# A two-layer graph network: layer 1 gives 25 chunks of gathered rows to the queues of SP and ScalarE instead of 38

## The chip, the cores and the metric

One core of a Trainium2 chip runs the whole program. The metric is the device time of one execution in microseconds, the median of several. The engines are TensorE (PE, matmuls), VectorE (DVE), ScalarE (ACT), GpSimd (POOL) and SyncE (SP), each with its own instruction queue, and 16 DMA engines which move what SP, ScalarE and GpSimd issue.

## The reference

3750 nodes with 256 features, 120,000 edges sorted by their target, 8 edge types. Layer 0 is a graph attention layer and layer 1 a relational one. Cut to layer 1, on which the change works:

```
h    = relu(layernorm(x))                    # 3750 x 256
W    = einsum('rb,bio->rio', comp, basis)    # 8 types
hall = einsum('ni,rio->nro', h, W)           # 30000 rows of 256 floats: tab1
msgs = hall[src, type]                       # 120000 gathered rows
agg  = segment_sum(msgs, dst)                # sum per target node
x    = x + layernorm(gelu(agg + h @ loop_w + bias + h)) * gamma + beta
```

## The kernel before

The nodes are 30 blocks of 128. The edges, sorted by target block, are cut into chunks of 128; layer 1 has `SLOTS` = 120000 // 128 + 30 = 967 chunks in groups of `G` = 32. For each chunk the 128 rows of `tab1` (1 KB each) are brought to the 128 partitions, and TensorE multiplies them with a one-hot matrix of the targets (`OH`), which sums them per target node. Chunks are taken in units of two, those from 936 on singly. After each unit VectorE adds the PSUM bank to the accumulator of the target's block (`add`, L1361), whose offset it has in a register.

Rows come in one of two ways. For most chunks GpSimd issues one indirect DMA (`fetch`, L867 to L882) into `FE`, which has room for two groups. Before every eighth chunk it waits until TensorE is done with the eight that lay there (L877), so it runs at most 56 to 64 chunks ahead. For the chunks in `BY_SP` and `BY_ACT` (L21, L22) the rows are copied one at a time by SP or ScalarE: `row_loads` (L518) loads 16 row addresses into registers with one register load (L526) and issues one DMA of 1 KB for each (L531), eight times for a chunk. They go to six tiles of their own, three for each queue (`QROWS`, named `qs` and `qa`). A chunk may be started when the one three before it in its list has been multiplied. `fetch` leaves these chunks out. TensorE takes all chunks in order and waits for each one's semaphore (L2110 to L2122).

SP does nothing but `row_loads` in this stage, all 128 rows of a chunk after those of the last (L773). ScalarE has other work between: for each node block b (one to a group of chunks) it makes `HXL` (L1826) and the next block's `relu` (`own_rows`, L1812), and then issues its share of register loads (L1829). TensorE multiplies block b with `loop_w` behind unit 11 of group b (`own_product`, chunk 24 of the group), for which it needs that `HXL`. ScalarE's first chunk is issued whole ahead of block 0's `HXL` (L1821).

Layer 0 gives chunks to the same queues by its own rule (`direct0`, `row_loads0`), which the change doesn't touch.

Of the kernel before, what the change touches and what calls it, by code (L numbers as in the profile page):

```python
# [17 lines left out]
GROUPS1 = [(k, min(G, SLOTS - k)) for k in range(0, SLOTS, G)]  # L18
UNITS = [(k, 2) for k in range(0, TWOS, 2)] + [(k, 1) for k in range(TWOS, SLOTS)]
ENT = 2 * NB + 1  # L20
BY_SP = [47 * j + 46 for j in range(20)]  # L21
BY_ACT = [52 * j + 50 for j in range(18)]  # L22
ER, EC = 125, 960
PARTS = (slice(0, 112), slice(112, ER))
EP = E + 128
# [20 lines left out]
def program(nc, x, src, dst, et, w0, al, ar, hb0, basis, comp, loopw, hb1, gam, bet, out):  # L46
# [15 lines left out]
    with ctx:  # L62
# [368 lines left out]
        def all_scored(g):  # L431

            return scored(g, halves(g) - 1)
# [29 lines left out]
        def direct(k):  # L463

            return k in BY_SP or k in BY_ACT

        def place_of(k):

            by = BY_SP if k in BY_SP else BY_ACT
            i = by.index(k)  # L470
            return 3 * (by is BY_ACT) + i % 3, i // 3

# [45 lines left out]
        def row_loads(e, engine, by, i, first, last):  # L518


            c = by[i]
            slot, use = place_of(c)
            if i >= 3 and first == 0:
                e.wait_ge(s_pair, NPAIR + unit_of(by[i - 3]) + 1)
            for p in range(first, last, 16):
                at = nc.values_load_multi_w_load_instructions(  # L526
                    ROWKEY[c % 128:c % 128 + 1, c // 128 * 128 + p:c // 128 * 128 + p + 16], engines=[engine],
                    min_val=0, max_val=4 * D * (NB * 128 * NREL - 1), skip_runtime_bounds_check_because=
                    "a key is 8 times a node plus a type, or one of the padding's below 30000, times the bytes of a row")[1]
                for r, v in enumerate(at):  # L530
                    e.dma_start(QROWS[slot][p + r:p + r + 1, :].bitcast(U8), bytes1[:, bass.ds(v, 4 * D)]).then_inc(d_q[slot], 16)  # L531
# [61 lines left out]
        def _(sp):  # L593
# [178 lines left out]
            sp.wait_ge(s_sc, all_scored(NG - 1))  # L772
            for i in range(len(BY_SP)):  # L773
                row_loads(sp, SYE, BY_SP, i, 0, 128)

# [888 lines left out]
        def _(ac):  # L1664
# [36 lines left out]
            for layer in range(2):  # L1701
# [9 lines left out]
                for j in range(4 if layer == 0 else 0):  # L1711
                    n = slice(512 * j, 512 * j + 512)
# [68 lines left out]
                for g in range(NG):  # L1781
                    k0, n = GROUPS[g]
# [25 lines left out]
            def own_rows(b):  # L1808

                if b:  # L1810
                    ac.wait_ge(s_tr, 2 * NB + b)
                ac.activation(ERM[:, 0:256], X[:, b, :], ACT.Relu, bias=nmr[:, b:b + 1], scale=rs[:, b:b + 1]).then_inc(*o.of(s_h))  # L1812
# [7 lines left out]
            ac.wait_ge(s_ef, NG)  # L1820
            row_loads(ac, SE, BY_ACT, 0, 0, 128)  # L1821
            for b in range(NB):
                ac.wait_ge(s_hm, 2 * NB + b + 1)
                if b:
                    ac.wait_ge(s_mm, 9 * NB + b)
                ac.activation(HXL[:, 0, :], ERM[:, 256:512], ACT.Copy).then_inc(*o.of(s_hi))  # L1826
                if b + 1 < NB:
                    own_rows(b + 1)
                for n in range(8 + 5 * b, min(13 + 5 * b, 8 * len(BY_ACT))):  # L1829
                    row_loads(ac, SE, BY_ACT, n // 8, n % 8 * 16, n % 8 * 16 + 16)  # L1830

            ac.activation(sm[:, 0, 0:1], ones[:, 0:1], ACT.Gelu).then_inc(*o.of())
# [325 lines left out]
```

## Time and profile before

| | us |
|---|---|
| median of 3 runs | 4180.63 (4178.63 to 4185.44) |
| the profiled execution | 4177.85 |
| its span, first to last instruction | 4175.4 |
| layer 1's first gather | 2214.6 |
| SP's last chunk of rows multiplied from | 4116.86 |

| engine | busy us | share of the span |
|---|---|---|
| PE | 1996.9 | 48% |
| PE weight load | 1520.2 | 36% |
| DVE | 1602.5 | 38% |
| ACT | 588.0 | 14% |
| POOL | 1984.0 | 48% |

Busy time doesn't count instructions that issue DMAs or load registers, so the table says nothing of SP. The mean granted TensorE clock is 0.687 of full speed.

### The profile page before, as it was taken

To read this page: it belongs to the slowest core of one execution; us is meant where nothing else is said; L and a number is where in the kernel's file an instruction comes from. 1 tells how busy PE (TensorE), PEld (TensorE's weight loads), DVE (VectorE), ACT (ScalarE), POOL (GpSimd) and SP (SyncE) were. 2 spreads that over 40 slices of the span, in tenths; PEclk is the share of its full clock that TensorE was granted. 3 is DMA by queue.
4 is the path that set the end of the run, shared out by engine and by line. 5 is a ranking of instruction groups with operands and counts; after the bars stand their busy time and mean duration, and the time that the engine had idled before them with its cause. 6 is when DMAs were issued, how large, how long until landed. Compare 5 with 4: busy or idle time off the path is not lost.

```text
span 4175.4 us, 44278 instructions
## 1 busy us (share of the span) xinstructions
PE 1996.9 (48%) x8319; PEld 1520.2 (36%) x8319; DVE 1602.5 (38%) x3360; ACT 588.0 (14%) x1181; POOL 1984.0 (48%) x2091
## 2 busy tenths in 40 slices
PE   8843555555555555555893243333233332323334
PEld 7832434333344343333682133222222222222223
DVE  6744445444544455445772122212122122211224
ACT  5332111122211122221250000000000000000003
POOL 6654555555555554554205445444344454534441
PEclk9966767666666676676896566566566666666667
DMA  8453333333333333333354222222122222222221
GB/s 237 169 184 89 104 101 102 100 91 107 105 104 103 102 104 88 102 107 86 131 184 130 65 68 77 65 69 68 51 63 72 68 75 67 74 57 61 63 68 47
DMA packets 185625, 397.95 MB, mean 95 GB/s; under 512 B 54570, under 2 KB 109666, under 8 KB 177024
## 3 DMA queue, kind: packets, MB, share of 16 engines
q0 software_dynamic: 92096, 252.73, 22.1%
q1 hardware_dynamic: 84800, 138.01, 9.9%
q10 hardware_dynamic: 8448, 4.37, 0.5%
q14 instruction: 215, 1.76, 0.1%
q8 instruction: 66, 1.08, 0.1%
HBM read 320.39 MB, written 74.55 MB: 95 GB/s over the span
## 4 chain that ended last, share of the span: by engine, by line
SPq 28%; issue 26%; PE 19%; DVE 11%; another core or an unknown queue 10%; ACTq 3%; ACT 1%; DVEq 1%; DMA 0%; POOL 0%; POOLq 0%
SPq L531 24%; PE PB L1947 9%; PE PB L1890 7%; SPq L526 4%; DVE ZX L1389 4%; DVE OHZ L1379 3%; ACTq L507 2%; DVE ACC L1361 2%; PE PB L1999 1%; DVE ERM L1370 1%; DVEq L1337 1%; PE PB L2050 0%; ACTq L502 0%; DVE EV L1405 0%
## 5 line engine op out<-in xcount | busy, mean ns | idle before, releaser
L882 POOL DMA_INDIRECT ZX<-tab,KI x1896 | 1809.3, 954 | 2012.8 <-PE PB L1947 1075.8
L1947 PE MATMUL PB<-ZX,OHZ 128*128 128x260 f32 (+1 forms) x3850 | 1221.1, 476 | 573.6 <-issue 350.4
L1361 DVE TENSOR_TENSOR ACC<-ACC,PB 128x260 f32 (+1 forms) x997 | 421.7, 423 | 2152.5 <-PE PB L1947 1012.2
L1947 PEld LDWEIGHTS PB<-ZX,OHZ 128*128 128x128 f32 x3850 | 901.6, 243 | 811.7 <-issue 404.4
L1890 PE MATMUL PB<-wh,hx 128*128 128x512 f32 (+2 forms) x980 | 308.5, 387 | 11.2 <-ACT hx L1686 5.6
L1999 PE MATMUL PB<-OHZ,ERG 128*32 128x256 bf16 x1494 | 157.5, 337 | 324.6 <-issue 313.9
L1389 DVE TENSOR_TENSOR ZX<-ZX,PB 128x2048 f32<-128x2048 f32 (+1 forms) x125 | 284.1, 2273 | 0.0
L1826 ACT ACTIVATE hxl<-ERM 128x256 fp32r<-128x256 f32 x30 | 12.5, 416 | 1881.0 <-issue 1201.4
L1999 PEld LDWEIGHTS PB<-OHZ,ERG 128*32 128x32 bf16 x1494 | 67.7, 109 | 412.2 <-issue 398.0
L1890 PEld LDWEIGHTS PB<-wh,hx 128*128 128x128 f32 x980 | 190.6, 195 | 33.9 <-ACT hx L1686 10.0
L1890 PE MATMUL PB<-wx,hx 128*128 128x512 f32 (+2 forms) x490 | 186.9, 381 | 0.0
L1754 ACT ACTIVATE OHZ<-OHZ,kid 128x4096 bf16<-128x4096 bf16 (+1 forms) x32 | 115.7, 3615 | 490.1 <-issue 444.3
L2015 PE MATMUL PB<-pick,ERM 128*128 128x16 f32 (+1 forms) x504 | 112.9, 374 | 149.7 <-DVE ERM L1370 94.7
L2015 PEld LDWEIGHTS PB<-pick,ERM 128*128 128x128 f32 (+1 forms) x504 | 109.4, 329 | 170.0 <-DVE ERM L1370 106.8
L1890 PE MATMUL PB<-wlh,hxl 128*128 128x256 f32 x120 | 40.5, 395 | 270.0 <-ACT hxl L1826 268.2
L1947 PE MATMUL PB<-qs,OHZ 128*128 128x256 f32 x40 | 21.8, 647 | 306.2 <-DMA qs<-tab 269.1
L1379 DVE TENSOR_TENSOR OHZ<-DL,PB 128x1024 f32<-128x1024 bf16 (+1 forms) x122 | 140.1, 1209 | 0.1
L1578 DVE TENSOR_TENSOR OHZ<-DL,PB 128x4096 f32<-128x4096 bf16 (+1 forms) x31 | 133.4, 4307 | 0.0
L1890 PEld LDWEIGHTS PB<-wlh,hxl 128*128 128x128 f32 x120 | 27.5, 252 | 277.8 <-ACT hxl L1826 205.6
L1947 PEld LDWEIGHTS PB<-qs,OHZ 128*128 128x128 f32 x40 | 11.3, 314 | 313.2 <-DMA qs<-tab 232.9
L2098 PE MATMUL PB<-IDX,ERM 128*128 128x128 f32 x30 | 12.0, 401 | 217.6 <-DVE ACC L1605 134.5
L1756 ACT ACTIVATE OHZ<-OHZ,ones 128x4096 bf16<-128x4096 bf16 (+1 forms) x32 | 115.7, 3615 | 1.0
(336 smaller groups left out, 1735.6 us busy)
## 6 DMA issues: line engine op xcount, KB each, us to landing
qs<-tab SPq DMA_DIRECT2D x2560, 1.0 KB
qa<-tab ACTq DMA_DIRECT2D x2304, 1.0 KB
tab<-ZX SPq DMA_DIRECT2D x34, 1024.0 KB
OHZ<-dlt SPq DMA_DIRECT2D x31, 1024.0 KB
ZX<-tab ACTq DMA_DIRECT2D x1920, 1.0 KB
ZX<-tab,KI POOLq DMA_INDIRECT x1896
ZX<-tab SPq DMA_DIRECT2D x1792, 1.0 KB
tab<-ZX SPq DMA_DIRECT2D x24, 1040.0 KB
```

Source lines behind the costliest of these rows:

```text
L526: at = nc.values_load_multi_w_load_instructions(ROWKEY[c % 128:c % 128 + 1, c // 128 * 128 + p:c // 128 * 128 + p + 16], engines=[engine], ...
L531: e.dma_start(QROWS[slot][p + r:p + r + 1, :].bitcast(U8), bytes1[:, bass.ds(v, 4 * D)]).then_inc(d_q[slot], 16)
L882: pool.indirect_dma_start(to, None, tab, at).then_inc(d_fe[g % 2][part(g, k) * layer], 16)
L1361: dv.tensor_tensor(a, a, bank(done + i)[:, 0:width], ALU.add).wait_op(*previous, "sem-ge").then_inc(*o.of(s_add))
L1379: dv.tensor_tensor(OH[:, 0, c:c + w, :], DL[:, k0 + c:k0 + c + w].unsqueeze(2).to_broadcast([128, w, 128]), (iob[:, :] if c and g == NG - ...
L1389: dv.tensor_tensor(f, f, weights.unsqueeze(3).to_broadcast([128, w, 4, HD]), ALU.mult).then_inc(*o.of(s_sr))
L1578: dv.tensor_tensor(OH[:, g % 2, 0:n, :], DL[:, k0:k0 + n].unsqueeze(2).to_broadcast([128, n, 128]), lanes.unsqueeze(1).to_broadcast([128, ...
L1754: ac.activation(d, d, ACT.Abs, bias=kid[:, 0:1], scale=-1.0).then_inc(*o.of())
L1890: last = pe.matmul(to, hx[:, 128 * c:128 * c + 128], parts[u](c), start=(i == 0 and c == 0 and u == 0), stop=(i == 1 and c == 1))
L1947: last = pe.matmul(p, OH[:, slot, k + i, :], rows_, start=(i == 0), stop=(i == n - 1))
L1999: last = pe.matmul(PB[2 + half][32 * a:32 * a + 32, 256 * (m % 2):256 * (m % 2) + 256], ERG[:, q, 32 * i:32 * i + 32], DLB[:, g % 2, 2 * q ...
L2015: last = pe.matmul(to, ERM[0:32 * parts, 128 * j:128 * j + 128], pick[0:32 * parts, 0:4 * parts].rearrange("p (a h) -> p a h", h=4), start ...
```

## The change

`BY_SP` has 13 chunks, 69, 141, ... 933, where it had 20 (46, 93, ... 939); `BY_ACT` has 12, 56, 132, ... 892, where it had 18 (50, 102, ... 934). The 13 chunks that neither list holds any more are fetched by GpSimd, 942 gathers instead of 929. ScalarE's register loads of 16 rows are dealt out to the blocks at three and four in turn instead of five; its first chunk is still issued ahead of block 0. All else, the tiles and the rules for waits among it, follows from the two lists.

```diff
-BY_SP = [47 * j + 46 for j in range(20)]
-BY_ACT = [52 * j + 50 for j in range(18)]
+BY_SP = [72 * j + 69 for j in range(13)]
+BY_ACT = [76 * j + 56 for j in range(12)]
...
-                for n in range(8 + 5 * b, min(13 + 5 * b, 8 * len(BY_ACT))):
+                for n in range(8 + 7 * b // 2, min(8 + 7 * (b + 1) // 2, 8 * len(BY_ACT))):
                     row_loads(ac, SE, BY_ACT, n // 8, n % 8 * 16, n % 8 * 16 + 16)
```

## Rows read from the trace of the kernel before

**Rows 1.** The page's chain that ended last, by engine (q is an engine's queue)
```profile
SPq 28%; issue 26%; PE 19%; DVE 11%; another core or an unknown queue 10%; ACTq 3%; ACT 1%; DVEq 1%; DMA 0%; POOL 0%; POOLq 0%
```
**Rows 2.** The chain of waits from 2357 to 4116 us, by line
```profile
by line: SPq L531 53.6%; issue 37.7%; SPq L526 8.7%; DMA qs<-tab 0.1%
```
**Rows 3.** The page's DMA issues (out<-in, count, KB); timeline of SP (start, us, count)
```profile
qs<-tab SPq DMA_DIRECT2D x2560, 1.0 KB
qa<-tab ACTq DMA_DIRECT2D x2304, 1.0 KB
...
2215.06 1900.44 SPq L531 DMA_DIRECT2D qs<-tab  x2560
```
**Rows 4.** Waits from 2300 us on: engine, line, releaser, us, times, longest
```profile
POOL ZX L882 <- PE PB L1947: 605.9, 33, 34.3
PE PB L1947 <- DMA qs<-tab: 450.8, 15, 41.6
...
PE PB L1890 <- ACT hxl L1826: 268.2, 9, 67.9
...
POOL ZX L882 <- remote: 106.1, 30, 12.3
```
**Rows 5.** Lines L531, L882, L1361 from 2225 to 2310 us (count, ns min/median/max, starts)
```profile
L531 SPq DMA_DIRECT2D qs<-tab x31: 5/702/1398, 2224.9 to 2309.9; - x31
...
L882 POOL DMA_INDIRECT ZX<-tab,KI x68: 956/956/961, 2224.8 to 2309.3; - x68
...
L1361 DVE TENSOR_TENSOR ACC<-ACC,PB x9: 420/421/422, 2228.6 to 2306.6; 128x256 f32 x9
```
**Rows 6.** The same lines from 2857 to 2921 us
```profile
L531 SPq DMA_DIRECT2D qs<-tab x58: 3/214/728, 2856.8 to 2920.7; - x58
...
L531 ACTq DMA_DIRECT2D qa<-tab x56: 3/214/737, 2856.8 to 2920.0; - x56
...
L882 POOL DMA_INDIRECT ZX<-tab,KI x46: 954/960/965, 2856.6 to 2919.5; - x46
...
L1361 DVE TENSOR_TENSOR ACC<-ACC,PB x20: 420/420/424, 2861.6 to 2906.8; 128x256 f32 x20
```
**Rows 7.** Line L531 from 2922 to 2945 us
```profile
L531 SPq DMA_DIRECT2D qs<-tab x54: 3/228/303, 2922.1 to 2944.4; - x54
L531 ACTq DMA_DIRECT2D qa<-tab x42: 3/214/701, 2921.4 to 2939.1; - x42
```
**Rows 8.** Line L531 on SP in the three runs of gathers of that stretch
```profile
L531 SPq DMA_DIRECT2D qs<-tab x18: 3/15/728, 2856.8 to 2876.8; - x18
...
L531 SPq DMA_DIRECT2D qs<-tab x16: 10/208/728, 2880.0 to 2897.3; - x16
...
L531 SPq DMA_DIRECT2D qs<-tab x17: 3/228/718, 2900.6 to 2917.9; - x17
```
**Rows 9.** Line L882, from 2215 to 2357 us and from there on
```profile
L882 POOL DMA_INDIRECT ZX<-tab,KI x86: 956/956/1025, 2214.6 to 2333.9; - x86
...
L882 POOL DMA_INDIRECT ZX<-tab,KI x843: 953/960/974, 2361.9 to 4080.0; - x169
```
**Rows 10.** Timeline of ScalarE, first and last `relu` of 2354 to 2581 us (of 5)
```profile
2354.14 0.59 ACT L1812 ACTIVATE ERM<-X,nmr,rs 128x256 f32<-128x256 f32 x1
...
2580.24 0.58 ACT L1812 ACTIVATE ERM<-X,nmr,rs 128x256 f32<-128x256 f32 x1
```
**Rows 11.** Timeline of TensorE: start, us, operation, count, idle before and releaser
```profile
2354.49 0.55 PE L1890 MATMUL PB<-wlh,hxl 128*128 128x256 f32 x1 [67.92 <-ACT hxl L1826]
...
4116.86 1.22 PE L1947 MATMUL PB<-qs,OHZ 128*128 128x256 f32 x2 [26.29 <-DMA qs<-tab]
...
4122.06 9.23 PE L1947 MATMUL PB<-ZX,OHZ 128*128 128x256 f32 x42
```

## The prediction

> **What bounds the kernel now.** I read the chain of waits first. Over the whole span it says only that SP's queue has the largest share, 28% [rows 1]. Cut to layer 1's aggregation, from 2357 us (SP's first chunk done) to 4116 us (its last), the same view has nothing but SP: L531, its row copies, 53.6%, the time between them 37.7%, and the register loads of L526 8.7% [rows 2]. SP issues its 2560 row copies without a break from 2215.06 for 1900.44 us [rows 3]. So layer 1 lasts as long as SP needs for its 20 chunks. The view of waits gives the other side: TensorE stands 450.8 us in 15 waits for `qs`, the tiles that SP fills, and 268.2 us in 9 waits for the `hxl` copy that ScalarE makes only after its own row copies; GpSimd stands 605.9 us waiting for TensorE, because its two groups of buffers are full [rows 4]. GpSimd is idle because of SP; it is not the bound.
>
> **What a row copy costs depends on GpSimd.** From 2225 to 2310 us GpSimd issues 68 gathers back to back, one per 1.26 us, and SP gets 31 rows through in 85 us: 0.36 a us [rows 5]. From 2922 to 2945 us GpSimd stands, and SP issues 54 rows in 23 us: 2.35 a us, ScalarE 42 in 17.7 us, 2.37 a us [rows 7]. The usual stretch of work lies between: 2857 to 2921 us holds 46 gathers (48 chunks less one each of SP and ScalarE) in three runs with short pauses between them (106.1 us in 30 such pauses in all, 3.5 us each [rows 4]), and SP issues 58 rows in 64 us: 0.91 a us, ScalarE 56 [rows 6]. It does not sink within that stretch: its three runs of gathers, 17 to 20 us each, hold 18, 16 and 17 rows [rows 8]. All these counts hold the register loads in them, which therefore need no term of their own.
>
> That gives a budget for SP: rows issued = 0.91 a us while GpSimd works at the stretch's pace (64 us for 46 gathers) + 2.35 a us while it stands. I test it on before. Behind SP's first chunk 843 gathers are issued [rows 9], 843 x 64/46 = 1173 us, in which 1067 rows go. SP still has 19 x 128 = 2432, so 1365 are left, 1365/2.35 = 581 us. Sum 1754 us; the trace has 1759 (2357 to 4116). The budget holds within 5 us.
>
> **The change, part by part.**
> *SP: 20 chunks become 13.* 896 row copies and 56 register loads go from SP's queue. Nothing else is queued there until the output.
> *Up to 2357 us nothing changes.* SP's and ScalarE's first chunks are again 128 rows each from 2215 us, and GpSimd's first stretch has two chunks left out of it as before (56 and 69, where it was 46 and 50). TensorE stands at chunk 24 (the own product of group 0) until ScalarE has issued its 128 rows: 2354.49 us, after 67.92 us of waiting [rows 11]. I cost this part at nothing.
> *GpSimd: 13 gathers more,* 942 for 929. By themselves 13 x 64/46 = 18 us of working time. They lie in time in which GpSimd stands now, and I count them in the budget.
> *SP's budget after.* 942 - 86 = 856 gathers are left behind 2357 us [rows 9]; 856 x 64/46 = 1191 us, in which 0.91 x 1191 = 1084 rows go. 12 x 128 = 1536 are needed; 452 are left, 452/2.35 = 192 us of standing GpSimd. Sum 1383 us: SP's last chunk lands at 2357 + 1383 = 3740 us, where it was 4116.
> *ScalarE: 18 chunks become 12, five register loads (80 rows) per group become three and four in turn.* In its first groups ScalarE is the one that holds TensorE: its `relu` pieces start at 2354.14, 2412.86, 2470.68, 2527.21 and 2580.24 us, a mean of 56.5 us a group [rows 10]. One and a half loads fewer are 24 rows; the working time of GpSimd in a group stays, so they come out of its standing time, at 2.37 a us: 10.1 us. That leaves 46.4 us a group. SP's budget asks for 72/32 = 2.25 groups a chunk, 1383/12 = 115 us, or 51.2 us a group, so ScalarE is about 5 us a group earlier than SP and is hidden by it. Without that cover it would still not take longer than SP.
> *The tail.* From SP's last chunk to the end it is 4175.4 - 4116.86 = 58.5 us [rows 11]. After the change 33 chunks lie behind SP's last (933), for 27 behind 939; six more at the 9.23 us for 21 chunks of the same rows are 2.6 us. 61 us.
> *Sum.* 3740 + 61 = 3801 us of span. A group with four loads takes ScalarE half a load longer than the mean, 8/2.37 = 3.4 us, inside the 5 us of cover; I add 5 us in all for starts that don't fit. The profiled execution took 4177.85 us for a span of 4175.4, 2.4 us more, and the median is 2.8 us above it. 3801 + 5 + 5 = 3811: I say 3810 us.
> *Bounds of what isn't shown.* Before has no stretch of work longer than 64 us between two waits for SP except the first; after, 70 gathers (97 us) lie between two chunks of SP. The rate of rows in such a stretch is between 0.36 [rows 5] and, if the shorter waits pull the gathers apart, something over 0.91; I take 0.91, because [rows 8] show no fall and the short pauses come back all through the stage.
>
> The Trainium skill ("DMA: Bandwidth & Descriptors", Issuing engine by pattern) says that copies issued from the sync and scalar queues are generally faster than those of GpSimd and leaves indirect ones to GpSimd. Read as a rule for this change it would speak against it. Here the unit is a chunk of 128 rows: one gather of 1.26 us on GpSimd, against 128 copies and 93 us on SP, so the trace decides against the rule's first half.
>
> **Rivals.**
> *A. Long stretches starve the row copies.* If the rate falls to 0.6 a us in 97 us stretches, 1191 us hold 715 rows and 821 are left, 349 us: 1540 us, SP's last chunk at 3897, the end at 3897 + 61 + 10 = 3968 us. At 0.36 throughout it is 429 and 1107 rows, 1662 us, 4090 us: still faster than now. For it: the first stretch. Against it: [rows 8], and the starving of VectorE in a long stretch itself brings the pauses.
> *B. SP falls out of the chain; ScalarE's loop and the gathers' pace are what is left.* 25 groups at 46.4 us from 2356 reach chunk 824 at 3516 us; the 109 chunks up to 933 at 64/48 = 1.33 us a chunk end at 3661; with 61 and 5 us, 3727 us. For it: the two budgets are only 5 us a group apart, and SP starts with its first chunk done when TensorE stands 45 chunks ahead of needing it. Against it: SP is busy in every microsecond of the chain now, and its rows are counted.
> *C. Slower: VectorE's adds take the place.* In the first stretch VectorE starts 9 adds in 78 us, 9.75 us each [rows 5], in the usual one 20 from 2861.6 to 2906.8 us, 2.4 us each [rows 6]; each add has register work ahead of it. A group has 16 adds and takes 63 us now (1759 us for 893 chunks). It decides from a mean of 3.9 us an add, that is when over a fifth of them are starved (2.4 + 7.35 x 0.21). At three in ten it is 4.6 x 16 = 74 us a group, 28.4 groups from 2356: 2100 us, the end at about 4520 us. Against it: TensorE stays a steady distance behind GpSimd in the stretches now, and what is starved stops the gathers, which frees it.
> [...]
>
> **Chances.** Forecast 0.55, A 0.20, B 0.20, C 0.03, and 0.02 that something else holds the time. 0.2% is about what a measurement of this kernel tells from no change; all cases but C and the last are far beyond it: faster 0.95, within 0.02, slower 0.03. The range 3715 to 3960 us holds the forecast, nearly all of B and the nearer half of A.
>
> **What would show it.** Right: SP's row copies run without a break from 2215 to about 3740 us, at some 115 us a chunk; the chain between is SP's alone; GpSimd's idle time for TensorE falls from 606 to some 190 us; VectorE's adds still come each 2.4 us in stretches; ScalarE's groups come each 46 to 52 us. A stretch of over 80 us with fewer than 0.7 rows a us shows A. TensorE's waits for `qs` gone and those for `hxl` left show B. Adds 9 us apart for whole groups show C. The forecast is wrong if SP's queue has breaks or if the first chunk ends elsewhere than at 2357 us.

## The result and the profile after

3835.97 us median (3828.74 to 3840.19, 4 runs) against 4179.63 us: ratio 0.9171, 95% interval 0.9155 to 0.9187. The change makes the kernel 344 us faster; 3810 was predicted, 370 us faster. A second pair, run later, gave 3830.26 against 4176.76 us, ratio 0.9163 (0.914 to 0.9186). But of the six sets of experiments four fell on chips on which the kernel before takes some 2920 us, and there the same split of chunks (with ScalarE's rows dealt out evenly, e7_even) is no gain but a loss of 0.6%. Both are told below; the traces of this section are of the changed kernel in its first result.

The profiled execution took 3828.74 us, its span 3827.1. The chain of waits from 2360 to 3760 us, between SP's first chunk and its last, is still SP's alone (for [rows 2]):

```profile
by line: SPq L531 50.9%; issue 43.3%; SPq L526 5.8%
```

The timeline of SP (start, us, count), for [rows 3]:

```profile
2208.85 1552.01 SPq L531 DMA_DIRECT2D qs<-tab  x1664
```

The waits from 2300 us on (engine, line, releaser, us, times, longest), for [rows 4]:

```profile
POOL ZX L882 <- PE PB L1947: 241.5, 26, 25.6
PE PB L1890 <- ACT hxl L1826: 230.7, 9, 65.8
...
PE PB L1947 <- DMA qs<-tab: 197.5, 9, 32.7
...
POOL ZX L882 <- remote: 128.5, 36, 11.8
```

GpSimd's idle time for TensorE fell from 605.9 to 241.5 us, TensorE's for `qs` from 450.8 to 197.5; the waits for ScalarE's `hxl` hardly fell, 268.2 and 230.7. The first stretch, 2225 to 2310 us, is much as it was, for [rows 5]; one row copy is two steps, a MOVE of a register and the DMA, and both take 700 ns in the median:

```profile
L531 SPq MOVE qs<-tab x30: 6/700/709, 2225.6 to 2308.9; - x30
...
L531 SPq DMA_DIRECT2D qs<-tab x29: 5/700/709, 2227.0 to 2307.5; - x29
...
L882 POOL DMA_INDIRECT ZX<-tab,KI x65: 952/957/961, 2224.9 to 2305.7; - x65
...
L1361 DVE TENSOR_TENSOR ACC<-ACC,PB x7: 420/420/420, 2228.6 to 2301.4; 128x256 f32 x7
```

And a stretch of work like that of [rows 6], 3097 to 3209 us, most of one chunk of SP (120 of 128 rows): the row copies and the gathers, and two of the five longer idle times of GpSimd ahead of a gather in it (timeline):

```profile
L531 SPq DMA_DIRECT2D qs<-tab x120: 3/228/1385, 3097.1 to 3208.9; - x120
...
L882 POOL DMA_INDIRECT ZX<-tab,KI x70: 953/957/974, 3099.5 to 3198.9; - x70
```
```profile
3099.51 0.96 POOL L882 DMA_INDIRECT ZX<-tab,KI  x1 [16.41 <-PE PB L1947]
3121.61 0.95 POOL L882 DMA_INDIRECT ZX<-tab,KI  x1 [3.48 <-remote]
```

One long wait for TensorE (16.4 us) stands in these 112 us, and four short pauses of 3.2 to 3.5 us (the other three ahead of the gathers at 3143.40, 3166.64 and 3190.02 us). Over all twelve chunks behind SP's first, a chunk took 117.5 us with 20 us of waiting for TensorE (241.5/12); the forecast had said 115 and 16 us (192/12).

### The profile page after: what moved, and what is told of

It is laid out like the page before. It is cut to its first block, busy times and chain, and to the rows that moved or that the text cites. A ratio compares the mean times of both kernels' runs of the same rounds, so it can differ in the third digit from the quotient of the medians.

```text
span 3827.1 us, 40843 instructions
## 1 busy us (share of the span) xinstructions
PE 1984.1 (52%) x8319; PEld 1512.6 (40%) x8319; DVE 1602.1 (42%) x3360; ACT 588.3 (15%) x1181; POOL 1993.7 (52%) x2104
## 4 chain that ended last, share of the span: by engine, by line
issue 29%; SPq 24%; PE 21%; DVE 11%; another core or an unknown queue 8%; ACTq 4%; ACT 2%; DVEq 1%; POOL 0%; DMA 0%; POOLq 0%
SPq L531 21%; PE PB L1947 11%; PE PB L1890 7%; ACTq L507 4%; DVE ZX L1389 3%; DVE OHZ L1379 2%; SPq L526 2%; PE PB L1999 2%; DVE ACC L1361 1%; DVE ERM L1370 1%; SPq L507 1%; ACTq L502 1%; DVEq L1337 1%; ACT ERG L1768 0%
## 5 line engine op out<-in xcount | busy, mean ns | idle before, releaser
L882 POOL DMA_INDIRECT ZX<-tab,KI x1909 | 1819.6, 953 | 1673.5 <-PE PB L1947 714.3
L1361 DVE TENSOR_TENSOR ACC<-ACC,PB 128x260 f32 (+1 forms) x997 | 421.4, 423 | 1810.3 <-remote 923.5
L1999 PE MATMUL PB<-OHZ,ERG 128*32 128x256 bf16 x1494 | 149.4, 330 | 304.4 <-issue 304.2
L1890 PE MATMUL PB<-wlh,hxl 128*128 128x256 f32 x120 | 41.0, 398 | 270.1 <-ACT hxl L1826 230.7
L2098 PE MATMUL PB<-IDX,ERM 128*128 128x128 f32 x30 | 12.1, 404 | 203.2 <-DVE ACC L1605 111.7
L1768 ACT ACTIVATE ERG<-ER 128x96 bf16 x498 | 89.3, 267 | 177.8 <-PE PB L1999 173.6
```

What stands on the lines that cost most here:

```text
L882: pool.indirect_dma_start(to, None, tab, at).then_inc(d_fe[g % 2][part(g, k) * layer], 16)
L1361: dv.tensor_tensor(a, a, bank(done + i)[:, 0:width], ALU.add).wait_op(*previous, "sem-ge").then_inc(*o.of(s_add))
L1890: last = pe.matmul(to, hx[:, 128 * c:128 * c + 128], parts[u](c), start=(i == 0 and c == 0 and u == 0), stop=(i == 1 and c == 1))
L1999: last = pe.matmul(PB[2 + half][32 * a:32 * a + 32, 256 * (m % 2):256 * (m % 2) + 256], ERG[:, q, 32 * i:32 * i + 32], DLB[:, g % 2, 2 * q ...
```

## The experiments

Twelve experiments ran, in six sets, each set on one chip with the kernel before beside it. Where the kernel before takes 4130 to 4180 us I write condition A (the expectations call it the slow condition), where it takes 2916 to 2924 us condition B (their fast condition). Condition A was met on two chips (and in the first result), B on three, one of them twice. No chip was met in both, but neither was a chip of A met a second time, so it isn't shown whether the condition belongs to the chip or to the moment. Which it would be was known only afterwards, so three of the lists ran twice in B and never in A. The ratios in B are within 2% of 1, but their intervals leave 1 out.

| kernel | chunks of SP + ScalarE | gathers | condition | median us | before us | ratio, 95% |
|---|---|---|---|---|---|---|
| e1_sp_only | 13 + 18 | 936 | B | 2930.96 | 2923.85 | 1.0024 (1.0008 to 1.004) |
| e2_act_only | 20 + 12 | 935 | B | 2931.2 | 2923.85 | 1.0023 (1.001 to 1.0036) |
| e3_none | 0 + 0 | 967 | B | 2971.31 | 2923.85 | 1.0157 (1.0122 to 1.0192) |
| e4_17 | 9 + 8 | 950 | B | 2950.74 | 2923.85 | 1.009 (1.0065 to 1.0116) |
| e5_after, the change | 13 + 12 | 942 | A | 3830.26 | 4176.76 | 0.9163 (0.914 to 0.9186) |
| e6_before, for its trace | 20 + 18 | 929 | A | 4179.14 | 4176.76 | one run |
| e7_even | 13 + 12 | 942 | B | 2937.18 | 2916.46 | 1.0063 (1.0042 to 1.0083) |
| e8_17 | 9 + 8 | 950 | B | 2946.02 | 2916.46 | 1.0096 (1.0078 to 1.0115) |
| e9_sp13 | 13 + 0 | 954 | A | 3728.07 | 4133.59 | 0.901 (0.8976 to 0.9044) |
| e10_sp20 | 20 + 0 | 947 | B | 2946.22 | 2918.7 | 1.0092 (1.0072 to 1.0112) |
| e11_none | 0 + 0 | 967 | B | 2970.5 | 2918.7 | 1.0173 (1.0156 to 1.019) |
| e12_sp_only | 13 + 18 | 936 | B | 2927.18 | 2916.94 | 1.0031 (1.0021 to 1.0041) |

The edits, against the changed kernel (the lists, and with them the number of register loads per block):

```diff
# e1_sp_only, e12_sp_only
-BY_ACT = [76 * j + 56 for j in range(12)]
+BY_ACT = [52 * j + 50 for j in range(18)]
-                for n in range(8 + 7 * b // 2, min(8 + 7 * (b + 1) // 2, 8 * len(BY_ACT))):
+                for n in range(8 + 5 * b, min(13 + 5 * b, 8 * len(BY_ACT))):
# e2_act_only
-BY_SP = [72 * j + 69 for j in range(13)]
-BY_ACT = [76 * j + 56 for j in range(12)]
+BY_SP = [47 * j + 46 for j in range(20)]
+BY_ACT = [76 * j + 56 for j in range(11)] + [894]
# e3_none, e11_none: both lists empty; e9_sp13: BY_ACT empty; e10_sp20: BY_ACT empty and
+BY_SP = [47 * j + 46 for j in range(20)]
# where BY_ACT is empty
-            row_loads(ac, SE, BY_ACT, 0, 0, 128)
# e4_17, e8_17
+BY_SP = [104 * j + 101 for j in range(9)]
+BY_ACT = [112 * j + 84 for j in range(8)]
+                for n in range(8 + 9 * b // 4, min(8 + 9 * (b + 1) // 4, 8 * len(BY_ACT))):
# e7_even, in row_loads and in ScalarE's loop
-                    ROWKEY[c % 128:c % 128 + 1, c // 128 * 128 + p:c // 128 * 128 + p + 16], engines=[engine],
+                    ROWKEY[c % 128:c % 128 + 1, c // 128 * 128 + p:c // 128 * 128 + min(p + 16, last)], engines=[engine],
...
-                for n in range(8 + 7 * b // 2, min(8 + 7 * (b + 1) // 2, 8 * len(BY_ACT))):
-                    row_loads(ac, SE, BY_ACT, n // 8, n % 8 * 16, n % 8 * 16 + 16)
+                at, end = 128 + 56 * b, min(184 + 56 * b, 128 * len(BY_ACT))
+                while at < end:
+                    n = min(16, end - at, 128 - at % 128)
+                    row_loads(ac, SE, BY_ACT, at // 128, at % 128, at % 128 + n)
+                    at += n
```

**The first set, meant to part the change, and its surprise.**

> SP's list is the new one (13 chunks), ScalarE's list and its five register loads per group are those of before (18 chunks): 31 chunks by rows, 936 gathers. Theory Q (each queue has a budget of its own; the slower of the two sets the time): SP's budget is the one of the change, 1383 us behind its first chunk, but ScalarE needs 56.5 us a group as in the first groups of before, 28.4 groups x 56.5 = 1605 us, so about 2350 + 1605 + 61 = 4016 us. Theory S (SP's rows alone set the time, ScalarE is hidden, as the prediction had it): 3836 us, like the change. Theory R (one budget shared by both queues: time goes with the sum of the rows): 3968 rows for 4864 before and 3200 after, 4180 - 344 x 896/1664 = 3995 us; the chain tells it from Q by who holds TensorE.

> ScalarE's list is the new one (12 chunks, the last at 894 and not 892, which SP holds) with three and four register loads in turn, SP's list is that of before (20 chunks): 32 chunks by rows, 935 gathers. Theory Q and theory S: SP still issues 2560 rows; 849 gathers behind its first chunk are 1181 us of work with 1075 rows, 1357 more at 2.35 a us are 577 us, 1758 us in all: no change, 4180 us within 15. Theory R (rows of both queues count against one budget): 4180 - 344 x 768/1664 = 4021 us.

> No chunk of layer 1 goes by rows: both lists are empty, 967 gathers. The budget's limit (gathers at the stretch's pace of 64 us for 46): 881 x 64/46 = 1226 us from 2350, then the drain and the tail, about 3640 us. Rival C of the prediction (VectorE's adds starve in endless stretches of gathers, 4.6 us and more an add): over 4400 us. Third possibility: without the row copies of SP and ScalarE the pauses between the gathers go too (1.27 us a gather): about 3530 us.

> 9 chunks for SP (every 104th), 8 for ScalarE (every 112th, nine register loads in four groups): 950 gathers. Theory Q with the rate of 0.91 rows a us in work: 869 gathers behind SP's first chunk are 1209 us of work, which hold 1100 rows, more than the 1024 that SP needs: SP falls out of the chain and GpSimd's pace is left, 2350 + 1209 + 61 = 3620 us. If the rate in work falls with the length of the stretches (rival A, 0.6 a us): 725 rows in 1209 us, 299 more are 127 us, 3747 us. If something else binds once SP is short (VectorE's adds): no gain over the change, 3836 us or more.

None of the theories was met: the medians lie between 2931 and 2971 us, that of the kernel before is 2924. Fewer chunks by rows, that is more gathers, cost time here: 935, 936, 950 and 967 gathers are +7.4, +7.1, +26.9 and +47.5 us over the 929 of before, 1.0 to 1.3 us for each one more.

**The second set: the changed kernel, and before for its trace.**

> The changed kernel itself, on the chip of these experiments, where the kernel before takes 2923.85 us and not 4180. In the four runs so far on it the times go with the number of gathers alone: 936, 935, 950 and 967 gathers cost +7, +7, +27 and +47 us over 929, about 1.26 us each, and GpSimd issues without a pause. Theory G (here GpSimd's gathers are the bound, nothing is starved): 13 more gathers are 16.4 us, 2940 us, ratio 1.0056. Theory P (the prediction's budget holds here too, in some smaller measure): faster than before, at the ratio seen first 2681 us. Should this call find the chip in the condition of the first result, both are void and the ratio is 0.917 again.

> The kernel before, for its trace in the condition in which the experiments run. Theory G: 2924 us; GpSimd issues its 929 gathers of layer 1 at 1.26 us each without a pause, SP's row copies go at 0.32 us each both during gathers and between them (2.8 us during them in the first trace), VectorE's adds come as TensorE delivers. What differs from the first trace names the thing that was starved there.

Both came out in condition A, with the times of the first result, on a chip other than that of the first set. So A and B are no property of a kernel: the kernel before takes 4177 us here and 2924 there. Its trace was to be that of B; it repeats [rows 5] instead (31 row copies in 85 us).

**Even shares of ScalarE, and 17 chunks once more.**

> The change with ScalarE's rows dealt out evenly: 56 rows (16, 16, 16 and 8, cut at the ends of chunks) for every block, where the change has 48 and 64 in turn. Same lists, 942 gathers. Where the row copies are slow (kernel before at 4177 us): theory Q (in the first twenty groups ScalarE and not SP holds TensorE, mean 48.6 us a group, 32 and 65 us in turn): the even share is 48 to 49 us a group, so little is won, 0 to 20 us, 3815 to 3836. Theory S (SP's rows alone set the time): no change, 3830. Theory U (the uneven share is what costs, a 64-row group lasts 65 us and a 48-row group can't give it back): 15 us less in every second of 20 groups, 3680 us. Where nothing is starved (kernel before at 2924 us) only gathers count: 942 are 13 more than before, 2940 us, for the change itself as well.

> 9 chunks for SP and 8 for ScalarE once more, 950 gathers; the first run of it was in the condition where nothing is starved. In the slow condition (before at 4177 us), theory Q with 0.91 rows a us in work: SP's 1024 rows fit into the 1209 us of work, GpSimd's pace is left, 2350 + 1209 + 61 = 3620 us. Rival A (0.6 rows a us in work): 3747 us. Rival C (VectorE's adds bind once the rows are few): 3836 us or more. In the fast condition 21 gathers more, 2950 us, as measured before.

Condition B again. e7_even has the change's lists and gathers, so its trace answers to that of the change. From 1800 to 1885 us, a stretch as long as that of [rows 5], with GpSimd at work throughout (count, ns min/median/max):

```profile
L531 SPq MOVE qs<-tab x206: 29/29/29, 1800.0 to 1885.0; - x103
L531 SPq DMA_DIRECT2D qs<-tab x205: 227/228/280, 1800.1 to 1884.7; - x103
...
L882 POOL DMA_INDIRECT ZX<-tab,KI x68: 956/960/969, 1800.0 to 1884.8; - x68
...
L1361 DVE TENSOR_TENSOR ACC<-ACC,PB x35: 420/421/423, 1800.3 to 1885.0; 128x256 f32 x35
```

The same 68 gathers of 0.96 us as in [rows 5], but 205 row copies where there were 31, and 35 adds where there were 9. The MOVE takes 29 ns each time, where its median is 700 in the first stretch of A, and the DMA's step 228 ns in the median for 700. That is what the two stretches differ in: in A the steps of SP's and ScalarE's queues and the adds of VectorE are held up, while the gathers keep their pace; in B nothing of the kind is seen. Layer 0 differs as well: its gathers run from 236 to 1973 us in the trace of before and from 225 to 1476 in that of e1_sp_only, so 486 of the 1254 us between these two spans lie there. Why one chip is held up and another isn't, no run shows. What bounds layer 1 changes with it; the chain of waits from 1800 to 2850 us and the waits of the stage:

```profile
by line: POOL ZX L882 75.9%; issue 24.1%
```
```profile
PE PB L1950 <- DMA ZX<-tab,KI: 297.9, 86, 7.1
POOL ZX L882 <- issue: 277.5, 910, 0.3
```

TensorE waits for gathers, and GpSimd for nothing but its 0.3 us between two. So a chunk given from SP to GpSimd costs its gather: 13 x 1.26 = 16.4 us for the change's lists, and e7_even is 20.7 us slower than before. The changed kernel itself was not run in B. The even share could not be judged, since in B ScalarE holds nobody. e8_17 repeats e4_17 (+29.6 and +26.9 us for 21 gathers). Both came out near what was expected for B, 2937 for 2940 us and 2946 for 2950.

**SP's 13 chunks alone.**

> SP's list is that of the change (13 chunks), ScalarE has none: 954 gathers, 12 more than the change. Slow condition (before at 4177 us): theory Q, a budget for each queue: SP needs as long as in the change, (954 - 81) x 64/46 = 1215 us of work with 1105 rows and 431 more rows at 2.35 a us, 183 us, 1398 us in all; ScalarE no longer holds TensorE in the first twenty groups, but SP was as slow: 2350 + 1398 + 61 = 3809 us, within 30 of the change's 3830. Theory R (both queues share one budget): ScalarE's 1536 rows are gone from it, SP's rate in work rises towards 1.7 a us, SP falls out of the chain, 2350 - 66 + 1215 + 61 = 3560 us (ScalarE's first 128 rows no longer hold TensorE at chunk 24 either). Fast condition (before at 2916 to 2924 us): only gathers count, 25 more than before, 31.5 us, 2948 to 2955 us.

Condition A, on another chip than the second set's, where the kernel before takes 4133.59 us: ratio 0.901, 1.5 points below the change's 0.9163, with intervals that don't touch but each against before on its own chip. Neither theory: 3728 us lies between 3809 and 3560. SP's timeline runs without a break for 1460.30 us, and the chain of waits from 2400 to 3660 us is its own (L531 50.9%, issue 42.5%, L526 6.6%):

```profile
2201.37 1460.30 SPq L531 DMA_DIRECT2D qs<-tab  x1664
```

SP's first chunk now ends at 2381 us, 31 us later than in the change: TensorE no longer stands for ScalarE at chunk 24, and GpSimd's second run of gathers has 24 where it had 8. The twelve behind it take 106.7 us each in the mean where they took 117.5. One of them, 3033 to 3138 us (count and starts), with 71 gathers where the 112 us of the change above hold 70:

```profile
L531 SPq DMA_DIRECT2D qs<-tab x127: 1/228/1402, 3032.9 to 3137.0; - x127
...
L882 POOL DMA_INDIRECT ZX<-tab,KI x71: 952/957/970, 3036.1 to 3135.1; - x71
```

In the unbroken first stretch, though, ScalarE's absence helps nobody (2225 to 2310 us, 30 rows for 31 and 29):

```profile
L531 SPq DMA_DIRECT2D qs<-tab x30: 13/700/1384, 2224.1 to 2306.7; - x30
```

So in such a stretch the queues don't divide one budget: SP's steps pass one per some 1400 ns, whether ScalarE issues or not. In the ordinary stretches it is otherwise: 11 us a chunk are gained. Two things differ there in the traces. The gathers come in more short runs (21 of 56 runs hold 8 or fewer, 7 of 58 in the change), in which SP's rows go faster; and in runs of the same length, 14 to 16 gathers, SP starts 1.12 rows a us for 0.83 with ScalarE's rows beside them. What lets SP go faster in runs of the same length isn't shown: it may be ScalarE's absence, or the shorter runs around them.

**Parting SP's list from ScalarE's, and no rows at all.**

> SP keeps its 20 chunks of before, ScalarE has none: 947 gathers. Slow condition: with the run of 13 chunks and none this parts the change into the share of SP's list and that of ScalarE's. Theory Q (SP's own budget, ScalarE's rows hardly touch it; in the run of 13 and none SP's rate in work was 1.07 rows a us for 0.85 to 0.91 with ScalarE's beside it): (947 - 86) x 64/46 = 1198 us of work with 1282 rows, 1150 more at 2.35 are 489 us, 1687 us for 1759: 70 us less than before, ratio 0.983, so SP's list has four fifths of the change's gain. Theory R (one budget): without 2304 of 4864 rows over 300 us less, ratio under 0.93. Fast condition: 18 gathers more, 22.7 us, ratio 1.008.

> No chunk by rows, 967 gathers, once more; the first run of it was in the fast condition. Slow condition: nobody waits for rows, what is left is GpSimd's pace. If the pauses stay as in the run of 13 and none (some 0.2 us a gather beside 1.265): 967 x 1.465 = 1417 us from 2205, and 60 us behind it: 3680 us, ratio 0.885 to 0.89. If VectorE's adds, 9 to 11 us each in long stretches, take over (rival C): 16 adds a group at over 3.9 us, 4180 us and more, ratio over 1. Fast condition: 38 gathers more, ratio 1.016 as measured.

> 13 chunks for SP as in the change, 18 for ScalarE as before, 936 gathers; the first run of it was in the fast condition. Slow condition: theory S (SP's rows set the time, ScalarE is hidden, as the prediction had it): the change's ratio, 0.917. Theory Q (the slower of two queues): ScalarE stays at its 56.5 us a group, 28.4 groups, 2350 + 1605 + 61 = 4016 us, ratio 0.961, with ScalarE's hxl as TensorE's releaser and hardly a wait for qs. Theory R (one budget of rows): 0.956, but with SP's queue still the one in the chain. Fast condition: 7 gathers more, ratio 1.0024.

All three fell in condition B: +27.5 us for 18 gathers, +51.8 for 38 and +10.2 for 7. They put the price of a gather in B at 1.4 to 1.5 us, somewhat above the 1.26 us from one gather to the next, and say nothing of A. In A it stays open what either list alone would give, whether 17 chunks or none is better than 25, and with that whether rival C ever decides.

## Why the prediction was right, point by point

*What bounds the kernel.* Right for the chip it was read from: SP's queue is never empty from its first row to its last, before and after, and the stage ends with its last row. It is not a property of the program; in B the same program is bound by GpSimd. The chain of waits overstates it, though: a queue without a break is its own chain, whoever holds TensorE. From 2350 to 2984 us of the changed kernel TensorE waited 160.7 us for `hxl` and 23.8 for `qs`; only from there to 3760 us it is 4.2 and 164.2.

*The budget for SP.* It came out 28 us short, and part of that closeness is luck. SP's first chunk was issued by 2350 us (2357 expected, the stage began 6 us earlier: 2208.85 for 2215.06 us). By the sign that the prediction set itself (the first chunk ends elsewhere than at 2357 us) it would count as wrong; the stage's earlier start explains 6 of these 7 us. From there to 2208.85 + 1552.01 = 3760.9 us it is 1411 us, 1383 forecast. 856 gathers were left, as forecast. The tail was 3827.1 - 3760.9 = 66 us for 61. 7 us earlier, 28 and 5 us longer: 3827 for the 3801 of the sum, and with that 3836 for 3810. GpSimd stood for TensorE 241.5 us, 192 were forecast, and worked the other 1169.5, forecast 1191. With 2.35 rows a us in the one, the other had (1536 - 2.35 x 241.5)/1169.5 = 0.83 rows a us. The same reckoning on before, with 605.9 us of standing and 1153 of work in 1759, gives 0.87. So the test on before, which closed within 5 us, hid two misses: 20 us too much for the work (64/46 = 1.39 us a gather where the stage's mean was 1.37) and 25 us too little for the standing (0.91 rows a us where the mean was 0.87). With the pace at 1.37 and the rate left at 0.91 the forecast would have been 1371 us, 40 short instead of 28.

*What a row copy costs, and why one rate served both kernels.* The prediction took two rates, one while GpSimd gathers and one while it stands, and read from [rows 8] that the first does not sink. The traces show that it does sink, within each run of gathers, and that it lags. At the end of the first stretch of before GpSimd stands from 2312.8 to 2325.07 us, yet SP issues 4 rows from 2313 to 2324 us; from 2325 to 2335 us GpSimd gathers again and SP issues 18:

```profile
L531 SPq DMA_DIRECT2D qs<-tab x4: 688/698/1396, 2314.9 to 2323.3; - x4
...
L531 SPq DMA_DIRECT2D qs<-tab x18: 3/228/755, 2325.0 to 2334.5; - x18
...
L882 POOL DMA_INDIRECT ZX<-tab,KI x8: 956/960/960, 2325.1 to 2333.9; - x8
```

In the changed kernel the 16 gathers from 3143.40 to 3163.3 us hold 8, 4, 2 and 2 starts of SP's rows in their four quarters. Counted over all runs of gathers of either kernel, SP starts 1.7 to 1.8 rows a us in a run's first 2 us, 0.6 after 8 us and 0.4 after 16 us, as few as in the unbroken first stretch; when a run ends it takes 2 more us (10 to 12 behind the 78 or 79 gathers of the first stretch, in all five traces of A) until the rate is back above 2. So 0.91 is a mean over runs of about 16 gathers and the pauses between them, and it carried over because the runs kept their length: behind the first chunk before has no run of gathers over 16, and the change only one, of 23. 49 of the 61 runs before and 50 of the 58 after hold 14 to 16 gathers, at 0.84 and 0.83 rows a us. The 70 gathers in a row that the prediction called the bound of what isn't shown never came. That they would not was its guess (the short pauses come back), and it was right; that length doesn't matter was a misreading of [rows 8]. What builds up in a run and drains behind it, nothing in the traces names.

*ScalarE hidden behind SP by 5 us a group.* Wrong: in the first twelve groups it wasn't hidden. ScalarE's `hxl` still made TensorE wait 230.7 us in 9 waits, 65.8 of them at chunk 24 of the start, where nothing was to change. Its groups don't differ by a load's 6.8 us (16 rows at 2.37 a us): with 64 and 48 rows in turn most of the first twelve take some 65 and 33 us. The timeline of ScalarE, two of these groups, from 2380.46 to 2983.97 us, whose mean is 50.3 us and not 46.4:

```profile
2446.53 32.23 ACTq L531 DMA_DIRECT2D qa<-tab  x48
2478.86 0.42 ACT L1826 ACTIVATE hxl<-ERM 128x256 fp32r<-128x256 f32 x1 [32.75 <-issue]
2480.26 64.15 ACTq L531 DMA_DIRECT2D qa<-tab  x64
2544.51 0.42 ACT L1826 ACTIVATE hxl<-ERM 128x256 fp32r<-128x256 f32 x1 [64.74 <-issue]
```

A likely reading, not shown by a run: the 48 rows fall largely into time in which TensorE waits for `hxl` and GpSimd stands, the 64 into gathering. While TensorE waits for ScalarE, GpSimd stands and SP's rows go on, so the same standing serves both queues, and a wrong cover cost little. That was luck: the prediction had no term for it. That removing ScalarE's rows altogether still gains (e9) shows that they weren't free; how much of the change's 344 us comes from ScalarE's shorter list and how much from SP's, no run in A parts.

*Rival A* (longer stretches starve the rows) had its mechanism right, as the paragraph on the rate shows, but not its condition: such stretches didn't form. *Rival C:* VectorE's adds are starved in the first stretch as before (7 in 73 us), and behind it they are not without price: TensorE waited 64.8 us in 13 waits for them (31.2 us in 10 before), and 111.7 us in 15 for another add of VectorE, L1605 (134.5 in 20 before). They come every 3.1 us within the runs of 14 to 16 gathers, under the 3.9 us at which they would decide. *Rival B* did not come in A, and a part of its end state, GpSimd's pace alone, is what condition B shows in every trace.

*What no part of the prediction considered* is that the price on which all of it rests, 0.36 to 0.91 rows a us beside the gathers, belongs to a condition that other runs don't have. In B it is 2.4 a us (205 in 85 us); SP's rows then fit beside the gathers, GpSimd's pace is left, and 13 gathers more are 16 us more. The Trainium skill ("DMA: Bandwidth & Descriptors", Issuing engine by pattern) calls copies of the sync and scalar queues generally faster, and the prediction said that the trace decides against it. It doesn't: one gather of 128 rows against 128 copies (1.26 us against some 53 us even in B) is no comparison of like transfers, so no run here bears that rule out or refutes it. That the chunks are better off on the sync and scalar queues in B comes from those queues being otherwise idle.

## What to carry to other kernels

Before a split of work between queues is tuned, measure what one issue costs while the other queues are busy and while they stand, and write the split as a budget of the two rates; here it forecast 370 us of gain for a measured 344, with errors that partly cancelled. Count such a rate by the time since the other engine's last pause, not only as a mean over a stretch. Then look at whether that cost is the same on other chips: this split is worth 8% on one and, with ScalarE's rows dealt out evenly, loses 0.6% on another. A queue that alone makes up the chain of waits is relieved by giving its work to an engine that waits for it, even where that engine looks the busiest in the table of busy times.

## What the runs showed of the hardware that I had not expected

Two of five chips of the experiments ran the same program 41 to 43% longer (4177 and 4134 us for 2916 to 2924), at the same length of a gather (0.96 us). The mean granted TensorE clock of before is 0.69 there and 0.78 to 0.79 on the others; which of the two, the longer time or the lower clock, brings the other isn't shown. On these two, while GpSimd issues indirect DMAs in a long run, a register MOVE of SP's or ScalarE's queue takes 700 ns for 29, a row copy 2.7 us in all (31 in 85 us) for 0.4 (205 in 85 us), and VectorE starts an add, which has its address in a register, once in 10 to 12 us; the add's own 421 ns don't change. The register loads from SBUF have nearly the same median in both (1.17 to 1.29 us in A, 1.26 to 1.30 in B), but the four of the first stretch of the change show 0.7 us. The slowness is not there from the first gather of a run, and it outlasts the last one, by some 2 us behind a run of 16 gathers and by 10 to 12 us behind one of 78. After that, with GpSimd standing, the steps are as short on these chips as elsewhere (MOVE 29 ns, DMA 228 ns). What makes the difference between the chips is open: nothing in the traces names it.
